# Graph layer 1: one tile in 64 is fetched row by row by SyncE instead of by GpSimd's gather

## What is computed

```python
x = _layernorm(x + _L0_gnn_ref(x, src, dst, edge_weight, L0_gnn_W), axis=-1)
x = _layernorm(x + _L1_gnn_ref(x, edge_index, edge_attr_9, w0, w1, w2, w3, w4), axis=-1)
...
summand = _tensor_product(x[i], edge_attr, [w0, w1, w2, w3, w4])
out = jax.ops.segment_sum(summand, j, num_segments=x.shape[0])
```

## Time and profile before

| | us |
|---|---|
| median of 3 runs | 5430.4 (5423.53 to 5431.77) |
| profiled execution | 5413.4 |
| its span | 5411.6 |
| POOL busy, 3027 instructions | 2874.1 (53%) |
| PE busy (matmul records) | 3424.5 (63%) |
| PE weight loads busy | 2944.5 (54%) |
| DVE busy | 2197.5 (41%) |
| ACT busy | 1257.7 (23%) |

### The profile page before, as it was taken

One profiled execution on the slowest core, in us unless ns is written; L12 is line 12 of the kernel. 1 busy time (PEld: TensorE's weight loads), 2 busy tenths in 40 slices (PEclk: granted clock), 3 DMA queues, 4 the chain that ended last, 5 costly groups with the idle time before them and its releaser, 6 DMA issues.

```text
span 5411.6 us, 78648 instructions
## 1 busy us (share of the span) xinstructions
PE 3424.5 (63%) x21792; PEld 2944.5 (54%) x21794; DVE 2197.5 (41%) x4685; ACT 1257.7 (23%) x2065; POOL 2874.1 (53%) x3027
## 2 busy tenths in 40 slices
PE   2101888888888888666666666665666566666555
PEld 1000777777777777554555555554555455555444
DVE  8997554555555444522222222222222222222333
ACT  4433444444444444300000000000000000000111
POOL 4100544555545444366666666666666666666554
PEclk6555988999989888666666776666666776666777
DMA  1000111111111111211111111111111111111221
GB/s 47 10 16 38 35 34 34 35 37 37 35 34 36 34 34 32 87 47 46 46 47 46 46 47 46 47 46 47 47 46 46 47 46 47 47 46 55 61 62 49
DMA packets 111891, 234.09 MB, mean 43 GB/s; under 512 B 52082, under 2 KB 52226, under 8 KB 110674
## 3 DMA queue, kind: packets, MB, share of 16 engines
q0 software_dynamic: 96560, 200.21, 12.8%
q1 hardware_dynamic: 10658, 24.72, 1.4%
q10 hardware_dynamic: 4608, 8.39, 0.4%
HBM read 218.42 MB, written 8.40 MB: 42 GB/s over the span
## 4 chain that ended last, share of the span: by engine, by line
PE 30%; issue 17%; another core or an unknown queue 6%; DVE 3%; DVEq 2%; POOL 0%; DMA 0%; ACT 0%; ACTq 0%; POOLq 0%
PE quad L1581 12%; PE mixed L1596 12%; PE quad L1573 3%; PE attr_t L1555 3%; DVE group L1692 2%; DVEq L1692 0%; DVEq L1696 0%; DVE attr_hot L1678 0%; DVEq L1683 0%; POOL feat L1478 0%; DVEq L1687 0%; DVE hot L1672 0%; DVE stats L1712 0%; DVE z_t L1708 0%
## 5 line engine op out<-in xcount | busy, mean ns | idle before, releaser
L1478 POOL DMA_INDIRECT feat<-x,ids x2048 | 1938.4, 946 | 1195.8 <-issue 586.1
L1045 POOL DMA_INDIRECT l_feat<-in_x,id_of x896 | 846.9, 945 | 1159.0 <-PE l_pre L1152 469.1
L1692 DVE TENSOR_TENSOR group<-group,quad 128x504 f32 (+1 forms) x512 | 347.2, 678 | 2212.3 <-remote 1347.3
L1596 PE MATMUL mixed<-group,mix 128*128 128x192 f32 x2304 | 685.7, 483 | 746.2 <-DVE group L1692 429.0
L1581 PE MATMUL quad<-attr_hot,feat 128*128 128x144 f32 x4096 | 927.0, 380 | 272.0 <-issue 270.6
L1596 PEld LDWEIGHTS mixed<-group,mix 128*128 128x128 f32 x2304 | 645.7, 304 | 780.4 <-issue 621.7
L1581 PEld LDWEIGHTS quad<-attr_hot,feat 128*128 128x128 f32 x4096 | 762.9, 257 | 412.3 <-issue 411.2
L1129 PE MATMUL got<-x_near,far_w 128*128 128x128 bf16 x6912 | 521.0, 225 | 153.7 <-issue 78.6
L1516 ACT CAST ids<-src_col 128x8 int32 (+1 forms) x256 | 50.5, 197 | 2363.3 <-DMA feat<-x,ids 2335.2
L1129 PEld LDWEIGHTS got<-x_near,far_w 128*128 128x128 bf16 x6912 | 455.2, 101 | 166.8 <-issue 166.3
L940 DVE TENSOR_SCALAR far_w<-far_w,cst 128x640 bf16<-128x640 bf16 (+1 forms) x256 | 103.2, 403 | 832.0 <-ACT far_w L756 752.0
(11 more groups left out here) (266 smaller groups left out, 3480.6 us busy)
## 6 DMA issues: line engine op xcount, KB each, us to landing
feat<-x,ids POOLq DMA_INDIRECT x2048
l_feat<-in_x,id_of POOLq DMA_INDIRECT x896
attr_in<-in_edge_attr SPq DMA_DIRECT2D x129, 72.0 KB
norm_x<-in_x SPq DMA_DIRECT2D x16, 256.0 KB, 2.8
x<-norm_z ACTq DMA_DIRECT2D x16, 256.0 KB, 2.3
x_t<-x SPq DMA_DIRECT2D x15, 256.0 KB
out<-z_t ACTq DMA_DIRECT2D x15, 256.0 KB
keys<-far_keys SPq DMA_DIRECT2D x2, 512.0 KB, 3.2
```

What stands on the lines that cost most here:

```text
L1045: pool.indirect_dma_start(feat[:, landing % RING, :], None, x, bass.IndirectOffsetOnAxis(ap=id_of[s % 2][:, c:c + 1], axis=0)).then_inc(fe ...
L1478: pool.indirect_dma_start(feat[:, t, :], None, x1, bass.IndirectOffsetOnAxis(ap=ids[t // H][:, t % H:t % H + 1], axis=0),).then_inc(feat_i ...
L1596: last = nc.tensor.matmul(mixed[:, 0:GROUP_WIN], g.mix[:, m, :], group[z][:, m, :], start=(m == 0), stop=(m == NA - 1))
L1692: nc.vector.tensor_tensor(to, to, quad[:, q, 0:NA * QUAD_WIN].rearrange("p (m n) -> p m n", m=NA), ALU.add).then_inc(quad_added, 1)
```

## The change

In every fourth row (the row with z = 3 of a cycle of four, `CYCLE`), tile 15 is no longer gathered by GpSimd. SyncE fetches its 128 node rows one by one, each with a DMA of 512 bytes whose source address comes from a register, into `single[0]` or `single[1]`, one buffer for even cycles and one for odd. The node numbers of these tiles are loaded once, at the start, into one partition (`single_ids`); SyncE reads eight of them at a time into registers. The 128 fetches of a cycle are spread over its four rows, 32 behind each attribute load. Before a cycle SyncE waits on `feat_used` and clears the landing count of the buffer; `single_open` tells PE that it has been cleared. At that tile PE waits on `single_open` and for 128 x 16 landings, and multiplies from `single`. The counts on which PE and ScalarE wait for a landing (`landings`) are now counted within a pass, and at its end GpSimd subtracts them, behind waits of its own, and adds to `landings_cleared`. GpSimd's and ScalarE's loops now have four rows to a body, PE's and SyncE's eight. The rest of the diff is names and semaphores.

```diff
         word_f = sb("word_f", [P, TN // QUAD_TILES], F32)
         ids = [sb(f"ids{h}", [P, H], I32) for h in range(2)]
         feat = sb("feat", [P, R, D], F32)
+        single = [sb(f"single{i}", [P, D], F32) for i in range(2)]
+        single_ids = sb("single_ids", [1, RN // CYCLE * P], I32)
...
+        def gathered(z, t):
+            return t < R - 1 or z < CYCLE - 1
+
+        def landings(i, z, t):
+
+            per = sum(gathered(y, t) for y in range(CYCLE))
+            return i * (16 * per) + 16 * sum(gathered(y, t) for y in range(z + 1))
+
...
             sp.dma_start(x_last[:], batches(x1)[NE]).then_inc(x_last_here, 16)
+            def fetch_rows(i, odd, z):
+
+                for first in range(z * (P // CYCLE), (z + 1) * (P // CYCLE), 8):
+                    nodes = nc.values_load_multi_w_load_instructions(
+                        single_ids[0:1, bass.ds(i * P + first, 8)], engines=[mybir.EngineType.SP], min_val=0,
+                        max_val=g.N - 1,
+                        skip_runtime_bounds_check_because="every source is the number of a node")[1]
+                    for k in range(8):
+                        sp.dma_start(single[odd][first + k:first + k + 1, :], x1[bass.ds(nodes[k], 1), :]
+                                     ).then_inc(single_in[odd], 16)
+
+            def cycle(w, i, odd, begin=False):
+
+                if begin:
+                    sp.wait_ge(feat_used, w * (RN * R) + R)
+                else:
+                    sp.wait_ge(feat_used, w * (RN * R) + (i * (CYCLE * R) - (CYCLE - 1) * R))
+                sp.sem_inc(g.turn, 1)
+                sp.sem_clear(single_in[odd])
+                sp.sem_inc(single_open[odd], 1)
+                for z in range(CYCLE):
+                    r = i * CYCLE + z
+                    u = w * RN + r
+                    load_attr(u + 1, (r + 1) % RN if isinstance(r, int) else r + 1, (z + 1) % 2)
+                    if isinstance(r, int) and 0 <= r + 1 - EARLY < NE:
+                        load_x(w, r + 1 - EARLY)
+                    fetch_rows(i, odd, z)
+
+            tile_ids = src.rearrange("(r t e) -> r t e", t=R, e=P)
+            sp.dma_start(single_ids[:].rearrange("o (r e) -> o r e", e=P),
+                         tile_ids[CYCLE - 1:RN:CYCLE, R - 1, :].unsqueeze(0)).then_inc(ids_here, 16)
+            sp.wait_ge(ids_here, 16)
             with passes(sp) as w:
-                with sp.Fori(0, EARLY // 2) as i:
-                    load_attr(w * RN + i * 2 + 1, i * 2 + 1, 1)
-                    load_attr(w * RN + i * 2 + 2, i * 2 + 2, 0)
+                for odd in range(2):
+                    cycle(w, odd, odd, begin=True)
+                with sp.Fori(1, EARLY // (2 * CYCLE)) as k:
+                    for odd in range(2):
+                        cycle(w, k * 2 + odd, odd)
                 load_x(w, 0)
-                for r in range(EARLY, RN):
-                    load_attr(w * RN + r + 1, (r + 1) % RN, (r + 1) % 2)
-                    if r + 1 - EARLY < NE:
-                        load_x(w, r + 1 - EARLY)
+                for i in range(EARLY // CYCLE, RN // CYCLE):
+                    cycle(w, i, i % 2)
...
         def _(pool):
             with passes(pool) as w:
-                with pool.Fori(0, RN) as r:
-                    u = w * RN + r
-                    for q in range(R // Q):
-                        if q % 2 == 0:
-                            pool.wait_ge(ids_made, u * 2 + (q // 2 + 1))
-                        pool.wait_ge(feat_used, u * R + 4 * q + 4)
-                        pool.sem_inc(g.turn, 1)
-                        for t in range(Q * q, Q * q + Q):
-                            pool.indirect_dma_start(
-                                feat[:, t, :], None, x1,
-                                bass.IndirectOffsetOnAxis(ap=ids[t // H][:, t % H:t % H + 1], axis=0),
-                            ).then_inc(feat_in[t], 16)
-            passes_run = pool.value_load(g.n_pass[0:1, 1:2], min_val=1, max_val=g.PASSES1)
-            for t in range(R):
-                pool.wait_ge(feat_in[t], passes_run * (16 * RN))
+                with pool.Fori(0, RN // CYCLE) as i:
+                    for z in range(CYCLE):
+                        u = w * RN + i * CYCLE + z
+                        for q in range(R // Q):
+                            if q % 2 == 0:
+                                pool.wait_ge(ids_made, u * 2 + (q // 2 + 1))
+                            pool.wait_ge(feat_used, u * R + 4 * q + 4)
+                            pool.sem_inc(g.turn, 1)
+                            for t in range(Q * q, Q * q + Q):
+                                if gathered(z, t):
+                                    pool.indirect_dma_start(
+                                        feat[:, t, :], None, x1,
+                                        bass.IndirectOffsetOnAxis(ap=ids[t // H][:, t % H:t % H + 1], axis=0),
+                                    ).then_inc(feat_in[t], 16)
+                for t in range(R):
+                    pool.wait_ge(feat_in[t], landings(RN // CYCLE - 1, CYCLE - 1, t))
+                pool.wait_ge(feat_used, w * (RN * R) + (RN * R + R))
+                pool.wait_ge(ids_made, w * (RN * 2) + (RN * 2 + 2))
+                pool.sem_inc(g.turn, 1)
+                for some in (range(0, H), range(H, R)):
+                    pool.inc_swdge_sem([feat_in[t] for t in some],
+                                       [landings(RN // CYCLE - 1, CYCLE - 1, t) for t in some], mode="sub")
+                pool.sem_inc(landings_cleared, 1)
             pool.sem_inc(g.turn, 1)
...
             with passes(act) as w:
-                def clear_and_copy(r, z, e=None):
+                def clear_and_copy(i, z, e=None):
+                    r = i * CYCLE + z
                     u = w * RN + r
                     act.wait_ge(group_used, u + 1)
-                    nc.scalar.memzero(group[z][:]).then_inc(group_zero, 1)
+                    nc.scalar.memzero(group[z % 2][:]).then_inc(group_zero, 1)
                     for h in range(2):
                         for t in range(h * H, h * H + H):
-                            act.wait_ge(feat_in[t], u * 16 + 16)
+                            act.wait_ge(feat_in[t], landings(i, z, t))
                         nc.scalar.copy(ids[h][:], g.src_col[:, bass.ds(r * R + (R + h * H), H)]
                                        ).then_inc(ids_made, 1)
                         if h == 0 and e is not None:
                             normalize(w, e)
 
-                with act.Fori(0, EARLY // 2) as i:
-                    for z in range(2):
-                        clear_and_copy(i * 2 + z, z)
+                act.wait_ge(landings_cleared, w + 1)
+                act.sem_inc(g.turn, 1)
+                with act.Fori(0, EARLY // CYCLE) as i:
+                    for z in range(CYCLE):
+                        clear_and_copy(i, z)
...
                         bank = quad[:, q, 0:NA * QUAD_WIN].rearrange("p (m n) -> p m n", m=NA)
                         for t in range(Q * q, Q * q + Q):
                             off = offset_in(word, t % Q, TILE_BITS, QUAD_WIN - WIN)
-                            pe.wait_ge(feat_in[t], u * 16 + 16)
-                            nc.tensor.matmul(bank[:, :, bass.ds(off, WIN)], feat[:, t, :],
+                            rows = feat[:, t, :]
+                            if gathered(z, t):
+                                pe.wait_ge(feat_in[t], landings(i, z, t))
+                            else:
+                                rows = single[odd][:]
+                                half = i // 2 if isinstance(i, int) else k
+                                pe.wait_ge(single_open[odd], w * (RN // (2 * CYCLE)) + half + 1)
+                                pe.wait_ge(single_in[odd], 16 * P)
+                            nc.tensor.matmul(bank[:, :, bass.ds(off, WIN)], rows,
                                              attr_hot[t // H][:, t % H, :, :], start=False,
                                              stop=(t % Q == Q - 1), skip_group_check=True
                                              ).then_inc(feat_used, 1)
...
+                pe.wait_ge(landings_cleared, w + 1)
+                pe.sem_inc(g.turn, 1)
+                with pe.Fori(0, EARLY // (2 * CYCLE)) as k:
+                    for odd in range(2):
+                        for z in range(CYCLE):
+                            row(k * 2 + odd, odd, z)
                 for r in range(EARLY, RN):
-                    row(r, r % 2, w * (RN // 2) + (r // 2 + r % 2), batch_of(r))
+                    row(r // CYCLE, r // CYCLE % 2, r % CYCLE, batch_of(r))
```

22 lines of the change are left out of this document (13 added, 9 removed).

## The result

| | before | after |
|---|---|---|
| median | 5431.1 us (5423.5 to 5434.1, 4 runs) | 6289.8 us (6260.3 to 6303.1, 4 runs) |
| ratio | | 1.158, 95% interval 1.155 to 1.160 |
| profiled execution, its span | 5413.4, 5411.6 | 6290.0, 6288.1 |
| POOL busy | 2874.1 | 2848.0 |
| DVE busy | 2197.5 | 2202.5 |

The account below looks back on a forecast made before the run. The prediction took layer 1's loop rows to be bound by GpSimd's gather run plus a release of PE's signals following its end. Terms -31 and +1 gave -30 us, moving the 5430.4 median to 5400; range over all cases 5382 to 5560.

Parts of the forecast that it names:

- Gathers removed, -31 of 35: Layer 1 loop: 28 cycles each lose one gather of 1.25 us, 35.0 us, of which 31 credited; unrolled rows get nothing.
- SyncE's fetches added, 18.6 us a row: SyncE's 32 fetches at 0.47 us plus loads take 18.6 us a row, hidden under GpSimd's 23.7.
- Both signs of being wrong: PE standing at tile 15 behind SyncE's DMAs or at the attributes; loop rows all near SyncE's own 32 DMAs.
- The slower case among the rivals: Gathers stall SyncE's fetches, or PE is delayed: up to 29.8 us a row, 6120 us; chance 0.33, a third under 5500.
- It decides at 0.63 us a DMA: In the slower case, the stall decides the time once SyncE's mean DMA passes 0.63 us.
- SP's traffic delays PE's signals further, at 0.2 us a row, +25: Rest of the slower case: SyncE's traffic makes PE's signals later by 0.2 us a row, +25 us.
- Waits added, costs nothing: SyncE's wait before a cycle, with the attribute load queued behind, costs nothing; PE's wait for 128 landings has some 60 us in hand.
- Transfers paid in parallel: SyncE's DMAs overlap their 2.4 us landings, so only issue time counts; one after another they would take 77 us a row.
- Loops, start and end, +1: Longer loop bodies lie under slack (0.3 us of SyncE a row); start loads and end waits cost 0 to 3 us, taken as 1.
- The lateness of PE's signals: In loop rows PE's mixing signals come about 1.5 us after the last gather's landing, 7.6 us after its modelled end; cause unknown.

Follow-up runs that it names:

- e1: Changed kernel without SyncE's fetches, tile 15 of every fourth row multiplied from fixed rows: 5383.3 us, ratio 0.993 to the kernel before.
- e3: Changed kernel with CYCLE 8, one tile in 128 and 16 fetches a row, on the chip without the stall: 4358.6 us, ratio 0.996 to before.
- e9: Changed kernel without fetches in the hardware loop; SyncE instead loads 32 node numbers a row one by one, no DMA: 6377.1 us, ratio 1.186 to before.
- e4: Changed kernel with 32 fixed rows fetched per row, one instruction each, no node numbers loaded: 5746.3 us, ratio 1.062 to before.
- e2: Changed kernel with all 16 tiles gathered again and SyncE's fetches going into buffers nobody reads: 6276.6 us in one run.
- e5: Fixed rows fetched by one instruction each, SyncE's loop body doubled from eight to sixteen rows: 5764.7 us, ratio 1.064 to before.
- e14: Changed kernel with all 32 fetches a row on ScalarE, 16 behind the clearing, 16 behind the first cast: 5702.3 us, ratio 1.062 to before.
- e17: Changed kernel with one tile in 128, 8 fetches by SyncE behind the attribute load, 8 by ScalarE behind the clearing: 5649.4 us, ratio 1.053 to before.
- e13: Changed kernel with one tile in 128, all 16 fetches a row by ScalarE between its casts: 5437.2 us, ratio 1.012 to before.
- e11: Changed kernel with CYCLE 8, one tile in 128 and 16 fetches a row by SyncE, on a stalling chip: 5652.7 us, ratio 1.052 to before.
- e15: Changed kernel with each row's fetches shared, 16 by SyncE and 16 by ScalarE, on a stalling chip: 5666.6 us, ratio 1.053 to before.

## Why the prediction was wrong, point by point

*Gathers removed, -31 of 35.* Right: e1 measured -33, by shorter rows of fifteen gathers (22.7 us) as the sum had it.

*SyncE's fetches added, 18.6 us a row.* This step failed. The duration was well chosen for a quiet stretch: 0.32 plus gaps was priced at 0.47 us a fetch, and e3 on the chip without the stall shows 228 + 37 + 29 ns, with sixteen in 7.3 to 7.7 us, 0.46 to 0.48 each with the register loads among them. But it was applied to instructions that lie inside a gather run, where a fetch takes 2.0 us on the chip of the result, and four of the five chips of the experiments were like it. A row took 31.4 us, not 18.6. Both signs of being wrong that were set down came: PE at its tile-15 matmul behind SyncE's DMAs and at the attributes, and rows as long as SyncE's own work.

*The slower case among the rivals* named the mechanism, its place and nearly its size (29.8 us a row and 6120 us, measured 31.4 and 6290), at a chance of 0.33 of which only a part lay that high; the range ended at 5560. What I held against it was weak. SyncE's median of 324 ns comes from one attribute load a row, and in the loop rows all 109 of them start in POOL's gap (4024.43 in the row), so they don't sample the stall. ScalarE's 46 to 60 ns do come from runs, half of them: no sequencer instruction of ScalarE takes over 128 ns in the loop rows before, amid stalled ones of PE. But they are a few behind each wait, and they don't say what a long series does: with fetches ScalarE reaches 1384. The maxima were the rows to read: 1141 ns for SyncE, 711 for PE, 1393 for VectorE.

*It decides at 0.63 us a DMA.* Too narrow, in two ways. e9 shows that register operations count as much as DMAs, and a fetch is three instructions, to which the loads come. And e4 costs 363 us over e1 with SyncE 10 us a row ahead of its work. That part of the rival, "SP's traffic delays PE's signals further, at 0.2 us a row, +25", was mis-sized by more than ten times: it is a whole gap of about 3 us more, since a signal that has not come by the twelfth gather cuts the run.

*Waits added, costs nothing.* Wrong with the above: PE waits 538 us for tile 15 in the profile after. The attribute load queued behind the fetches, which I had named and priced at nothing, takes that wait over when nobody reads the fetched rows (459 us in e2), with the same total time.

*Transfers paid in parallel.* Right in what it denied: the landings aren't the price (e2, e9). The Trainium skill (DMA: Bandwidth & Descriptors, Rules for kernel authors), which says to coalesce small transfers, gave the better advice all the same. One DMA of 32 rows has a ratio of 0.992 and 32 DMAs of one row 1.062, on two stalling chips. By e9 what is saved is instructions of SyncE, not time per transfer, and gathered rows at 128 addresses can't be coalesced so.

*Loops, start and end, +1.* Right, within what e1 can tell. The body's length has no price that shows (e5).

*The lateness of PE's signals*, which I had left open, belongs with it. On the chip without the stall a row is 20.0 us of back-to-back gathers, so the 4.0 us by which the earlier trace rows exceed it go with the stall, in the kernel before already. That PE's signals are late because its own instructions stall fits in part; but in the row of the profile after no instruction of PE stalls while its signal is 13 us late, so that can't be all of it, and the cause stays open.

What stays open: what the step of 0.7 us is a step of, how SyncE's instructions make PE's signal late, and why one chip of five has no stall. The records show the step and that four engines (ScalarE with them in e14 and e17) are in it together; nothing here shows the resource.

## What to carry to other kernels

Price an added instruction by rows from the stretch it will stand in, and where only a few of its kind stand there read the maxima, not the median: on four of these five chips an instruction of SyncE, PE, VectorE or ScalarE in a longer series can take 0.7 or 1.4 us while GpSimd gathers, whatever it does. Beside a run of gathers an otherwise idle sequencer is not free: with SyncE's instructions in the run the signal that releases the rest of it came too late (e4: +363 us), and a load that others wait for must not stand behind them. Where such rows are dear, save instructions rather than bytes, and time a change on more than one chip when its price is of issue and not of work.

## What the runs showed of the hardware that was not expected

- The same program takes 4377.5 us on one chip and 5368 to 5431 in the other groups. Layer 0 shows it too: its last gather starts at 1727.7 us in e3 and at 2199.8 in the kernel before on the chip of its profile. Windows of layer 0 alone, e3 and before (777 gathers against 563):

```profile
600.00:1650.00 1050.00, 1046.28 (x11539) 1006.55 (x11538) 731.95 (x2273) 642.93 (x1109) 737.11 (x777) 1.00 0.17 49
```
```profile
600.00:1650.00 1050.00, 861.51 (x8364) 801.20 (x8362) 536.52 (x1650) 465.10 (x805) 531.51 (x563) 0.92 0.12 35
```

- The mean granted clock is lower on the stalling chip, 0.92 against 1.00 here and 0.67 against 0.76 in the loop rows, with PE less busy. Whether the clock has a part in the difference is not shown; 8 to 12% of a clock don't make 697 ns of a register operation's 37.
- On the stalling chips the price of the same number of fetches depends on who issues them and where in the program: 16 cost 1.2% behind ScalarE's first cast (e13), 5.2% on SyncE (e11) and 5.3% shared, 8 and 8, early in the run (e17). Which of the two it is no run separates.
- ScalarE's few sequencer instructions behind each wait take at most 128 ns in the loop rows of the kernel before, while PE's and VectorE's stall there; only in a long series do ScalarE's stall too (e13 to e15, e17).
